# A gathered-experts kernel: the normed row copied to a PSUM bank for the dots, and one similarity bank from head 1 on

## The reference

```python
q = einsum('bnd,de->bne', x, w_q)                  # 2 * 8 * 128 columns
q = (q - mean) * rsqrt(var + BN_EPS) * gamma + beta
sim = einsum('pbnhd,hkpd->pbnhk', q, keys)         # two halves, 8 heads, 128 keys
sx, ix = top_k(sim[0], 8); sy, iy = top_k(sim[1], 8)
scores, pk = top_k(all 64 sums sx + sy, 8)
indices = ix * 128 + iy at pk                      # 8 of 16384 experts per token and head
h = gelu_new(einsum('bnd,bnhkd->bnhk', x, down_embed[indices]))
out = einsum('bnhk,bnhkd->bnd', softmax(scores) * h, up_embed[indices])
```

## Time and profile before

| | us |
|---|---|
| median of 3 runs | 2750.73 (2749.47 to 2762.49) |
| the profiled execution | 2754.73 |
| its span, first to last instruction | 2752.9 |
| PE busy | 2358.8 (86%) |
| DVE busy | 1867.1 (68%) |
| ACT busy | 1176.9 (43%) |
| POOL busy | 1140.5 (41%) |
| first gather issued, at | 1384.4 |
| mean granted clock of PE | 0.944 |

### The profile page before, as it was taken

One profiled execution on the slowest core, in us unless ns is written; L12 is line 12 of the kernel. 1 busy time (PEld: TensorE's weight loads), 2 busy tenths in 40 slices (PEclk: granted clock), 3 DMA queues, 4 the chain that ended last, 5 costly groups with the idle time before them and its releaser, 6 DMA issues.

```text
span 2752.9 us, 37794 instructions
## 1 busy us (share of the span) xinstructions
PE 2358.8 (86%) x12444; PEld 1258.0 (46%) x12444; DVE 1867.1 (68%) x5474; ACT 1176.9 (43%) x3224; POOL 1140.5 (41%) x1082
## 2 busy tenths in 40 slices
PE   6899999999999999998859877888788788876667
PEld 3455565655556565555534433334333344332222
DVE  2577777768777776767567767676676676756554
ACT  1457473655747464665323333333233232332222
POOL 2121211112121111210056567676676666577665
PEclk9999999999999999999979999999899898998889
DMA  4000101010000101012179899999999999899998
GB/s 173 9 22 8 37 1 43 1 44 1 18 27 8 36 2 43 1 41 77 34 263 369 294 366 371 340 363 348 359 362 357 360 350 365 325 347 353 355 378 329
DMA packets 161954, 521.78 MB, mean 190 GB/s; under 512 B 17248, under 2 KB 27488, under 8 KB 161760
## 3 DMA queue, kind: packets, MB, share of 16 engines
q0 software_dynamic: 129024, 469.82, 45.3%
q1 hardware_dynamic: 31152, 48.03, 5.3%
q10 hardware_dynamic: 1584, 1.52, 0.2%
HBM read 508.30 MB, written 11.01 MB: 189 GB/s over the span
## 4 chain that ended last, share of the span: by engine, by line
PE 20%; DVE 11%; issue 9%; another core or an unknown queue 4%; POOL 3%; DMA 2%; DVEq 1%; ACT 1%; POOLq 0%; ACTq 0%
PE ps_o L1764 8%; PE ps_y L1764 7%; DVE e_rows L1910 6%; PE ps_s L1734 3%; POOL e_rows L1714 3%; DMA e_rows<-in_experts,e_idx 2%; PE ps_t L1747 1%; DVE acc L1900 1%; DVE e_at L1844 1%; DVE e_best_at L1824 1%; ACT e_diag L1992 1%; DVEq L1848 1%; DVE e_top L1838 0%; DVE e_best L1821 0%
## 5 line engine op out<-in xcount | busy, mean ns | idle before, releaser
L1714 POOL DMA_INDIRECT e_rows<-in_experts,e_idx x896 | 905.4, 1010 | 469.1 <-issue 290.0
L1910 DVE CUSTOM_DVE_ANT_0 e_rows<-e_rows,xn_all 128x512 f32<-128x512 f32 x896 | 567.8, 687 | 144.4 <-DMA e_rows<-in_experts,e_idx 107.7
L1764 PE MATMUL ps_y<-e_rows,e_diag 128*128 128x512 f32 x896 | 435.4, 634 | 140.3 <-issue 81.2
L1764 PE MATMUL ps_o<-e_rows,e_diag 128*128 128x512 f32 x896 | 434.8, 632 | 132.8 <-issue 84.8
L1992 ACT ACTIVATE e_diag<-ident_f,e_weight 128x128 f32<-128x128 f32 x896 | 286.4, 390 | 562.6 <-remote 189.5
L1764 PEld LDWEIGHTS ps_y<-e_rows,e_diag 128*128 128x128 f32 x896 | 178.0, 203 | 374.0 <-issue 342.5
L1764 PEld LDWEIGHTS ps_o<-e_rows,e_diag 128*128 128x128 f32 x896 | 177.1, 203 | 363.9 <-issue 330.6
L1096 DVE SCALAR_TENSOR_TENSOR ring<-ps_s,mask 112x750 f32<-112x750 f32 x248 | 224.9, 935 | 128.7 <-PE ps_s L600 109.5
L1310 ACT ACTIVATE ring<-ring,neg_max 112x750 f32<-112x750 f32 x248 | 226.8, 916 | 157.7 <-DVE neg_max L1106 157.3
L1106 DVE CUSTOM_DVE_ANT_0 ring<-ring,mask_bias 112x750 f32<-112x750 f32 x248 | 233.4, 989 | 0.0
L1987 ACT ACTIVATE e_active<-e_hidden 128x4 f32<-128x4 f32 x224 | 45.6, 204 | 356.6 <-DVE e_hidden L1910 155.7
(11 more groups left out here) (206 smaller groups left out, 3163.7 us busy)
## 6 DMA issues: line engine op xcount, KB each, us to landing
e_rows<-in_experts,e_idx POOLq DMA_INDIRECT x896
xn_t<-in_ctx_t SPq DMA_DIRECT2D x8, 1500.0 KB, 6.6
w_in<-in_ffn_wq SPq DMA_DIRECT2D x16, 256.0 KB, 7.9
acc<-in_x SPq DMA_DIRECT2D x8, 448.0 KB, 4.9
acc<-x_dram SPq DMA_DIRECT2D x7, 512.0 KB, 6.5
xn_all<-x2n_dram SPq DMA_DIRECT2D x7, 512.0 KB, 7.7
out<-acc SPq DMA_DIRECT2D x14, 256.0 KB
x_dram<-x SPq DMA_DIRECT2D x7, 448.0 KB, 3.1
```

Source lines behind the costliest of these rows:

```text
L1714: pool.indirect_dma_start(rows[:, v % RING, k, :], None, table[:, :], bass.IndirectOffsetOnAxis(ap=idx[:, e:e + 1], axis=0))\
L1764: mm = nc.tensor.matmul(ps_out[t % 2][:], diag[:, HU * (v % ND) + k, :], rows[:, v % RING, k, D:], start=(s == 0 and k == 0), stop=(s == S ...
L1910: last = nc.vector.tensor_tensor_reduce(down, down, xn_all[:, t, :], 1.0, 0.0, ALU.mult, ALU.add, hidden[:, b, k:k + 1])
```

## The change

ACT copies the normed rows of a tile (128x512 fp32) into the PSUM bank `ps_m[1]`, one copy for each tile of each head, right after the gelu of the tile before's second unit and ahead of that unit's diagonals. The dots read their second operand there. DVE waits at the first unit of each tile for the copy (`xn_here`). The bank being taken, all similarities from head 1 on go to `ps_m[0]`; match g then waits for search g-1 instead of g-2. Head 0's similarities still use both banks, and the first copy waits until they have all been searched. The wait on the late part of `xn_all` moves from DVE to ACT.

```diff
+        xn_here_at = ps_m[1]
+
+        def sims_bank(head, g):
+
+            return ps_m[g % 2] if head == 0 else ps_m[0]
...
-                if n >= 1 or g >= 2:
+                if head >= 1:
+                    pe.wait_ge(searched, NG * n + g)
+                elif n >= 1 or g >= 2:
                     pe.wait_ge(searched, NG * n + g - 1)
                 for i in group(g):
-                    mm = nc.tensor.matmul(ps_m[g % 2][:, (i % TPB) * NK:(i % TPB + 1) * NK],
+                    mm = nc.tensor.matmul(sims_bank(head, g)[:, (i % TPB) * NK:(i % TPB + 1) * NK],
...
                 def sims(i):
-                    return ps_m[g % 2][:, (i % TPB) * NK:(i % TPB + 1) * NK]
+                    return sims_bank(head, g)[:, (i % TPB) * NK:(i % TPB + 1) * NK]
...
-                if h == 0 and v == SPT * AHEAD_TILES:
-                    dve.wait_ge(x2_in, 32)
+                if s == 0:
+                    dve.wait_ge(xn_here, NTF * h + t + 1)
...
-                    last = nc.vector.tensor_tensor_reduce(down, down, xn_all[:, t, :], 1.0, 0.0, ALU.mult, ALU.add,
+                    last = nc.vector.tensor_tensor_reduce(down, down, xn_here_at[:], 1.0, 0.0, ALU.mult, ALU.add,
...
+            def rows_here(h, t):
+
+                if h == HF:
+                    return
+                if h == 0 and t == AHEAD_TILES:
+                    act.wait_ge(x2_in, 32)
+                nc.scalar.copy(xn_here_at[:], xn_all[:, t, :]).then_inc(xn_here, 1)
...
                 nc.scalar.activation(active[:, b, :], hidden[:, b, :], ACT.Gelu_apprx_tanh).then_inc(active_ready, 1)
+                if s == SPT - 1:
+                    rows_here(h + (t + 1) // NTF, (t + 1) % NTF)
                 act.wait_ge(weight_ready, NV * h + v + 1)
...
             first_head()
+            act.wait_ge(searched, 2 * NG)
+            rows_here(0, 0)
```

More of the change, by code:

```diff
@@ L1566, in build_experts @@
         rows_used = sem("rows_used")
+        xn_here = sem("xn_here")
         hidden_ready = sem("hidden_ready")
```

## The result

The changed kernel takes 2800.51 us in the median of 4 runs, the kernel before on the same chip 2756.61: ratio **1.016**, interval 1.013 to 1.019, slower by 44 us. The forecast was +12. The execution profiled is the longest of the four, 2816.22 us (span 2814.4), so its sums run some 15 us high.

The account below looks back on a forecast made before the run. DMA at 1.28 us a gather was taken as the bound, with POOL as close a limit at 1.31 us an issue. The terms -28 + 0 + 4 + 17 + 19 = +12 us on 2750.7 gave 2763 us, range 2712 to 2798.

Parts of the forecast that it names:

- The dots' operand: DVE's dots no longer read two SBUF tiles, so POOL's gather issues lose their 57 us of stretch: -28 us.
- The bound "0": Limit given for the dots' operand: no gain where POOL only reaches the full ring sooner; the other limit was -57.
- The one bank: PE's match waits for the search one group later, holding the current unit's sums and gather slots: +17 and +19 us.
- the head's end: Units 20 to 26 of a head: a late match carries to unit 24, whose slot POOL needs next: +17 us.
- The 19 us: Units 3 to 9 of a head: held units cost where DVE or ACT stalls, at five places: +19 us.
- rival B: The bank decides: match waits for search, PE idles holding slots, POOL's waits grow 60 us or more; 2795 us, chance 0.15.
- The copies: ScalarE gains 112 copies at 0.61 us, for which DVE may wait: +4 us, bounds 0 and 52.
- The dot itself: DVE's dot with a PSUM operand takes as long as before, 687 ns: 0 us; the skill's surcharge would add 58.
- A: The relief wins: the bank costs nothing, as POOL keeps DVE fed and PE a unit late; 2723 us, chance 0.33.
- C: No relief: the issues' stretch comes from something else in the dot, their mean stays 1010 ns; 2791 us, chance 0.07.
- The 114 us of lost DMA time: Expert stage, 1430 to 2740 us: DMA's mean share 0.94 against 1.03, all that a faster feed could win.

Follow-up runs that it names:

- e4: The changed kernel with only the first tile's rows copied into the PSUM bank, the other 111 copies left out; ratio 1.0125 to the kernel before, without pauses.
- e1: The kernel before with only the bank taken away, dots still reading SBUF, no copies; 2641.10 against 2610.58 us, ratio 1.0111, without pauses.
- e14: The changed kernel again, on the same chip as e13, with pauses; 2812.39 us, ratio 1.0162 to the kernel before.
- e13: The kernel before with only the bank taken away, run again with pauses; 2806.4 us, ratio 1.0147.
- e6: The kernel before with each search one DVE step sooner and nothing else; ratio 1.0026, without pauses.
- e3: The changed kernel with each search one DVE step sooner; ratio 1.0029 to the kernel before, without pauses.
- e5: The changed kernel once more, without pauses; ratio 1.0135 to the kernel before.
- e8: The changed kernel with slot numbers that run on across heads; ratio 0.999 to the kernel before, without pauses.
- e7: The kernel before with slot numbers that run on across heads; ratio 0.996, without pauses.
- e10: The kernel before with slot numbers running on across heads and gathers of half the bytes; ratio 0.988, with pauses.

## Why the prediction was wrong, point by point

- **"The dots' operand": -28 us. This step failed.** The stretch is real and vanished (1010 to 946 ns, 57.7 us of POOL). I priced it by POOL's mean pace of 1.31 us against DMA's 1.28, as if POOL's pace set the end through all 896 issues. Measured it is worth nothing: e4 against e1 (+4 us, intervals overlapping) without pauses, e14 against e13 (+4 us by the ratios, +6 by the medians, copies included) with them. What POOL saves it waits: its waits for slots rise from 91 to 136 us (e1, e4) and from 222 to 298 (e13, e14); and where DMA sets the pace, gathers land no sooner (from issue to landing 6.8 us in the median in e6, 8.4 in e3). The bound "0" in my own text was the right value. The earlier trace rows pointed to it: POOL waited 168 us for slots, three times what the relief could free. (The counts of 346 and 66 issues were off: by the start times 400 begin inside a dot, and 55 inside that add; the stretch of the 400 sums to 55 us, near the 57.)
- **"The one bank": +17 +19 = +36 us.** Right in size: alone it measured 1.0147, 41 us (35 by the medians), with pauses and 1.0111, 29 us, without. The mechanism, a waiting match that holds a unit and so its slots, is shown by e5 against e8; that PE's standing still costs nothing by itself, by e3 against e6 too. The split was off: without pauses the head's end is some 27 us, where 17 were forecast (e8 less e7 is 0.003 of 0.0135). The 19 us were read at places where an engine pauses (at 2443 us, ACT stands still for 10.37 us with "remote" as the releaser), so they can count only with pauses; no run measures them by themselves. I left out that PE, once idle, runs at half its clock, which rival B named: at the place of the earlier trace rows the granted clock was 0.50 and the projection took 3.19 us.
- **"The copies": +4 us.** Held as far as can be told: some 3 us, e5 less e4 on two chips, inside the intervals; DVE waited 5.9 us for them. A copy took 579 ns, where I took 608.
- **"The dot itself": 0.** Held, 682 against 687 ns. The Trainium skill's surcharge for PSUM (Perfetto Trace Analysis, Optimizing Scalar/DVE Operations: about 125 ns against about 60) is not seen in this trace.
- **The sum.** Without the -28 it is +40 us; measured +44.
- **The rivals.** A is refuted: the bank does cost, and the relief gives nothing back. B was right in its test (POOL's waits grew by 109 us, over the 60 that I had named) and in its rule, that groups should rotate through banks; its time, 2795 us, is what the ratio gives on the 2750.73 of the forecast (2794), but by another sum: +40 from the bank and the copies and no relief, where it had a larger loss by the bank and half the relief. C fell: the issues did shorten. (The 114 us of lost DMA time are 0.09/1.03 of 1310 us; 0.09 x 1310, as written, is 118.)

What stays open: the pauses themselves. They are no fixed property of a chip, since one chip met both conditions, but no run tells what an engine waits for there. Open too is how the bank's cost splits with pauses, and what the relief is worth where POOL is the limit.

## What to carry to other kernels

A relief of an engine that feeds a ring is worth something only while the ring has room and the queue behind it does too. Before pricing it, add up that engine's waits for slots and look whether DMA is full; where they exceed what the relief frees, zero is the first guess, as it was here (168 us against 57). A wait added to an engine that works its list in order costs by what is queued behind it and by who gets room from that: put finished work first, or let the step that it waits for come one step sooner. And a buffer that changes its numbering at a loop's end is shallower there than its size; price any lateness at that place in full.

## What the runs showed of the hardware that I had not expected

- An indirect gather's issue on POOL is held by a dot with two SBUF inputs until that dot ends, and not by one with an SBUF and a PSUM input. In the trace of the kernel before 145 issues begin in the first 0.4 us of a dot, and nine in ten of them end 0.805 to 0.814 us after the dot does, however early they began; those that begin after 0.5 us of the dot take 0.94 us, as without it. In the changed kernel an issue begun in the first 0.4 us of a dot takes 0.94 in the median. The mean of all fell from 1010 to 946 ns, the minimum is 932 in both.
- The same kernel took 2609 us in one condition and 2757 to 2772 in another, 6% apart and on one chip both. The traces of the longer condition have pauses of 4 to 10 us in DVE, ACT and PE that the others lack. They are there too when DMA is at 0.64 (e10: 11 on DVE, 67 us). In the condition without them DMA moved 393 GB/s over most of the stage in e3 and e6; with them 355 in the kernel before.
- PE after 7.92 us of idle time ran a projection in 3.19 us, at a granted clock of 0.50, that takes 1.67 at 1.00.
